# Four PSUM banks in turn for the outputs of every batch of a spectral block, and new homes for the small results that lived in the fourth

## The reference

```python
def spec(x, w1, w2, out_hw):             # rfft2, keep few modes, weight them, irfft2
    xf = rfft2(x, norm='forward')
    top = xf[..., :m1, :m2] * w1; bot = xf[..., H-m1:, :m2] * w2
    return irfft2(place(top, bot), s=out_hw, norm='forward')
def tno(xa):                             # each of 4 x 64 images of 256 x 256 on its own channel
    n = inorm(xa)
    k, q, v = spec(n, kw), spec(n, qw), spec(n, vw)     # 8 x 8 mode blocks
    att = softmax(q . k over the 64 images of a batch) @ v
    att = inorm(att) + xa
    a = inorm(att)
    mixed = inorm(spec(a, mix_w) + skip_w * a)          # 32 x 32 mode blocks
    return inorm(mixed) + att
x = x + tno(group_norm(x))               # x: (4, 64, 256, 256) float32, 32 groups over the columns
```

## Time and profile before

| what | value |
|---|---|
| time, median of 3 runs (lowest, highest) | 711.17 us (709.3, 713.19) |
| the profiled execution: its own time, its span | 708.26 us, 706.2 us |
| PE busy, PEld busy | 659.0 us (93%), 589.9 us (84%) |
| DVE, ACT, POOL busy | 485.6 (69%), 334.8 (47%), 356.8 us (51%) |
| mean granted TensorE clock | 0.979 of full |
| HBM read and written | 68.23 and 67.11 MB |
| `produce` of batches 1 to 3, first store to last landed load | 114.1, 115.5, 114.4 us |

### The profile page before, as it was taken

One profiled execution on the slowest core, in us unless ns is written; L12 is line 12 of the kernel. 1 busy time (PEld: TensorE's weight loads), 2 busy tenths in 40 slices (PEclk: granted clock), 3 DMA queues, 4 the chain that ended last, 5 costly groups with the idle time before them and its releaser, 6 DMA issues.

```text
span 706.2 us, 15104 instructions
## 1 busy us (share of the span) xinstructions
PE 659.0 (93%) x5772; PEld 589.9 (84%) x5772; DVE 485.6 (69%) x1099; ACT 334.8 (47%) x722; POOL 356.8 (51%) x430
## 2 busy tenths in 40 slices
PE   6999998999999998999999989899999999988796
PEld 6999898788888898878888889878888888986574
DVE  3566566678767676577777765867777766656787
ACT  5888041464666513255566633236466660424141
POOL 1700024968980003795993002398699000359995
PEclk9999899999999999999999999999999999999799
DMA  8990000799889500199788910059979970005567
GB/s 265 389 361 3 1 1 2 226 309 296 284 302 301 192 1 1 52 317 328 259 307 289 304 56 1 1 174 316 316 263 304 296 242 1 1 1 209 205 245 297
DMA packets 71687, 136.32 MB, mean 193 GB/s; under 512 B 5376, under 2 KB 5888, under 8 KB 71616
## 3 DMA queue, kind: packets, MB, share of 16 engines
q1 hardware_dynamic: 71616, 135.36, 56.3%
HBM read 68.23 MB, written 67.11 MB: 192 GB/s over the span
## 4 chain that ended last, share of the span: by engine, by line
PE 63%; DVE 14%; POOL 13%; DMA 3%; issue 3%; ACT 2%; SPq 1%; DVEq 0%; ACTq 0%; POOLq 0%
PE psY L306 27%; PE psP L361 13%; POOL X L744 9%; PE psP L417 4%; PE psY L327 4%; PE psT L343 4%; PE psP L327 3%; DVE X L796 3%; DVE Y L796 3%; DVE SQ L796 2%; DMA X<-in_x 2%; DMA out<-X 1%; DVE QP L832 1%; ACT SQ L515 1%; POOL ALPHA L737 1%
## 5 line engine op out<-in xcount | busy, mean ns | idle before, releaser
L744 POOL TENSOR_TENSOR X<-X,ALPHA 128x512 f32<-128x512 f32 x244 | 254.8, 1082 | 27.5 <-DVE IM L1032 25.5
L306 PE MATMUL psY<-FWD,X 128*128 128x128 f32 x2048 | 248.3, 280 | 6.8 <-DMA X<-in_x 6.8
L306 PEld LDWEIGHTS psY<-FWD,X 128*128 128x128 f32 x2048 | 236.7, 194 | 21.5 <-issue 19.1
L796 DVE TENSOR_TENSOR X<-X,psP 128x512 f32<-128x512 f32 x240 | 155.7, 684 | 73.6 <-PE psP L361 60.9
L832 DVE TENSOR_REDUCE QP<-SQ 128x32 f32<-128x512 f32 x256 | 161.8, 679 | 63.4 <-ACT SQ L515 42.2
L361 PE MATMUL psP<-INVW,T 64*128 64x256 f32 x960 | 147.4, 406 | 19.5 <-DVE X L796 16.1
L515 ACT ACTIVATE SQ<-X 128x512 f32<-128x512 f32 x256 | 147.1, 622 | 16.0 <-DVE Y L803 9.1
L722 POOL TENSOR_TENSOR Y<-Y,OMEGA 128x256 f32<-128x256 f32 x32 | 25.3, 790 | 249.6 <-ACT Y L519 249.3
L361 PEld LDWEIGHTS psP<-INVW,T 64*128 64x128 f32 x960 | 94.9, 190 | 51.3 <-issue 39.4
L537 ACT ACTIVATE T<-psT,BIA,SCL 128x256 f32<-128x256 f32 x128 | 65.3, 561 | 116.3 <-PE psT L343 105.3
L507 ACT ACTIVATE Y<-psY 128x512 f32<-128x512 f32 x128 | 76.0, 594 | 66.2 <-PE psY L306 65.6
(11 more groups left out here) (189 smaller groups left out, 463.3 us busy)
## 6 DMA issues: line engine op xcount, KB each, us to landing
X<-in_x SPq DMA_DIRECT2D x128, 512.0 KB, 5.2
out<-X SPq DMA_DIRECT2D x128, 512.0 KB, 4.1
INVH<-t_inv_h SPq DMA_DIRECT2D x1, 256.0 KB, 4.9
LW<-in_low_w SPq DMA_DIRECT2D x1, 204.0 KB, 3.4
GWT<-t_w SPq DMA_DIRECT2D x1, 192.0 KB, 4.9
FWD<-t_fwd SPq DMA_DIRECT2D x1, 128.0 KB, 2.2
INVW<-t_inv_w SPq DMA_DIRECT2D x1, 128.0 KB, 4.7
LM<-in_low_mix SPq DMA_DIRECT2D x1, 68.0 KB, 3.0
```

What stands on the lines that cost most here:

```text
L306: last = mm(psY[p % 2][:, (2 * i + c) * 128:(2 * i + c + 1) * 128], X[:, 2 * p + i, a, c * 128:(c + 1) * 128], FWD[:, a, :], start=a == 0, ...
L744: P.tensor_tensor(v, v, al, MUL).then_inc(x_scaled, 1)
L796: return V.tensor_tensor(out, a, b, op)
```

## The change

Outputs use psP0, psP1, psP2 and psB in turn in all batches, and `inverse_w(s)` waits for image 2s-3 (out_made 2s-2) from s = 2 on; `inverse_w(1)` waits for the first low additions, which read psB. The squares' sums move from psB to the last columns of psT1, with a wait on t_kept. The small results of the second part move from psB to psY1 (psY0 in the last batch). For that, `energy`, `spread` and `turn_low` move behind `inverse_h` in their rounds and wait on y_kept, and the second `forward` of the round after each waits until VectorE has read them. VectorE handles the second part after the third image of a round instead of the fourth. In `attend` the early statistics go to psB instead of psT1.

```diff
...
         psM = [psY[0], psY[1], psP[2]]
-        psTot, psSta, psZ = psT[0], psT[1], psP
+        psTot, psSta, psZ = psT[0], psB, psP
         psA, psQ = psT[1], psP[0]
-        psE = [psT[1], psB]
+        psS = psT[1][:, 480:496]
...
         def out_bank(b, n):
-            return (psP + [psY[0]])[n % 4] if b == B - 1 else psP[n % 3]
+            return (psP + [psB])[n % 4]
+
+        def second_bank(b):
+            return psY[1] if b < B - 1 else psY[0]
+
+        def coef_bank(b, part):
+            return second_bank(b) if part else psT[1]
+
+        def low_bank(b, part):
+            return second_bank(b) if part else psB
...
             q = n // 4 - 4
-            return psY[1][:, GROUPS * q:GROUPS * q + 1] if q < 6 else psB[:, GROUPS * (q - 6):GROUPS * (q - 6) + 1]
+            return psY[1][:, GROUPS * q:GROUPS * q + 1] if q < 6 else psY[0][:, GROUPS * (q - 6):GROUPS * (q - 6) + 1]
...
+                if nb:
+                    pe.wait_ge(t_kept, 32 * (nb - 1) + min(2 * (k + LAG + 1) + 2, 32))
...
                 quad = QP[:, 4 * (k % 2):4 * (k % 2) + 4, :].rearrange("p i g -> p (i g)")
-                mm(psB[:, 480 + k:481 + k], quad, ONES[:, 0:1], start=True, stop=True).then_inc(q_added, 1)
+                mm(psS[:, k:k + 1], quad, ONES[:, 0:1], start=True, stop=True).then_inc(q_added, 1)
...
                     pe.wait_ge(mode_weighted, 8 * b + 6)
-                if b == B - 1 and s == 1:
-                    pe.wait_ge(mode_weighted, 8 * b + 7)
-                    pe.wait_ge(powers, 8 * b + 7)
-                if s:
-                    pe.wait_ge(out_made, 64 * b + 2 * s - (2 if b == B - 1 else 1))
+                if s == 1:
+                    pe.wait_ge(d_added, 6 * b + 4)
+                if s > 1:
+                    pe.wait_ge(out_made, 64 * b + 2 * s - 2)
...
                 pe.wait_ge(energy_part, 10 * b + (6, 10)[part])
-                mm(psE[part][0:IMGS, 496:497], FPH, ONES[:, 0:1],
+                mm(coef_bank(b, part)[0:IMGS, 496:497], FPH, ONES[:, 0:1],
...
                 pe.wait_ge(coef_made, 2 * b + part + 1)
-                mm(psE[part][:, 320:416], SIDE[:, :], RC, start=True, stop=True)
-                mm(psE[part][:, 416:480], ONES[0:IMGS, :], E2, start=True, stop=True).then_inc(coef_spread, 1)
+                mm(coef_bank(b, part)[:, 320:416], SIDE[:, :], RC, start=True, stop=True)
+                mm(coef_bank(b, part)[:, 416:480], ONES[0:IMGS, :], E2, start=True, stop=True).then_inc(coef_spread, 1)
...
                 j0, j1 = (0, 4 * SPLIT) if part == 0 else (4 * SPLIT, 32)
-                wait_alone(d_made, 2 * b + part + 1, psB)
+                wait_alone(d_made, 2 * b + part + 1, low_bank(b, part))
...
                         for h in range(2):
-                            last = mm(psB[64 * h:64 * h + LU, col:16 * (j1 - j0):16], vals, EI[:, 2 * j0 + h:2 * j1:2],
+                            last = mm(low_bank(b, part)[64 * h:64 * h + LU, col:16 * (j1 - j0):16], vals, EI[:, 2 * j0 + h:2 * j1:2],
...
                         forward(b + 1, 2 * (u - LAG))
+                        if u == LAG + 1:
+                            pe.wait_ge(var_made, 2 * b + 2)
+                        if u == LAG + 4:
+                            pe.wait_ge(c2_kept, 2 * b + 2)
+                        if u == LAG + 5:
+                            pe.wait_ge(d_added, 6 * b + 6)
                         forward(b + 1, 2 * (u - LAG) + 1)
-                    if u == LAG:
-                        energy(b, 1)
-                    if u == LAG + 1:
-                        pe.wait_ge(var_made, 2 * b + 2)
-                    if u == LAG + 3:
-                        spread(b, 1)
-                    if u == LAG + 4:
-                        pe.wait_ge(c2_kept, 2 * b + 2)
-                        turn_low(b, 1)
-                    if u == LAG + 5:
-                        pe.wait_ge(d_added, 6 * b + 6)
...
                             inverse_h(b, u + 1)
+                        if new and u in (LAG, LAG + 3, LAG + 4):
+                            pe.wait_ge(y_kept, 32 * (b + 1) + 2 * (u - LAG) + 2)
+                        if u == LAG:
+                            energy(b, 1)
+                        if u == LAG + 3:
+                            spread(b, 1)
+                        if u == LAG + 4:
+                            turn_low(b, 1)
...
                     act.wait_ge(d_added, 6 * b + 6)
+                    act.wait_ge(powers, 8 * b + 8)
...
                 dve.wait_ge(q_added, 16 * b + 16)
-                step(V.tensor_reduce(SUMS[:, 2:3], psB[:, 480:496], AX.X, ADD))
+                step(V.tensor_reduce(SUMS[:, 2:3], psS, AX.X, ADD))
                 ts(TOT[:, 32:64], SEL[:, :], SUMS[:, 2:3], None, MUL).then_inc(totals_in, 1)
-                tt(PAD.rearrange("p (k i) -> p k i", i=4), over(psB[:, 480:481], [[1, 16], [0, 4]]),
+                tt(PAD.rearrange("p (k i) -> p k i", i=4), over(psS[:, 0:1], [[1, 16], [0, 4]]),
...
                 dve.wait_ge(energy_sum, 2 * b + part + 1)
-                step(ts(im(28), psE[part][0:IMGS, 496:497], im(30), 0.0, ADD, ALU.max))
+                step(ts(im(28), coef_bank(b, part)[0:IMGS, 496:497], im(30), 0.0, ADD, ALU.max))
...
                 p0, p1 = ((0, 4 * SPLIT), (4 * SPLIT, PAIRS))[part]
-                ps = psE[part]
+                ps = coef_bank(b, part)
...
                     s = S[rows, q0:q1, 0, :, :].rearrange("p q j (r v) -> p q (j r) v", r=2)[:, :, :, 0:LV]
-                    d = psB[rows, 32 * (q0 - base):32 * (q1 - base)].rearrange("p (q n v) -> p q n v", n=4, v=LV)
+                    d = low_bank(b, n > 1)[rows, 32 * (q0 - base):32 * (q1 - base)].rearrange("p (q n v) -> p q n v", n=4, v=LV)
...
                             finish(b, n)
-                            if n % 4 == (3 if more else 1):
+                            if n % 4 == (2 if more else 1):
...
             def second_part(b, u, more):
```

## The result

| | before | after |
|---|---|---|
| time, median of 4 runs of each side by side | 711.08 us (709.3 to 713.19) | 690.75 us (687.99 to 692.2) |
| ratio, 95% interval | | 0.971 (0.966 to 0.975) |
| profiled execution: time, span | 708.26, 706.2 us | 689.49, 687.4 us |
| `produce` of batches 1 to 3, first store to last landed load | 114.0, 115.4, 114.4 us | 108.1, 109.9, 109.3 us |
| last batch, first store to the end | 70.05 us | 68.62 us |

The forecast was 695.5 us. The two profiled executions are 18.8 us apart: 16.5 in the three `produce` stages, 1.4 in the last batch, and 0.8 before the first store of batch 1 (at 126.5 against 127.3 us), which the change doesn't aim at. The three later `attend` stages take 165.0 us together in both.

The account below looks back on a forecast made before the run. TensorE, busy 93%, was taken as bound by its order and the joint's wait, with transfers second. Terms summed to 15.6 us: 692.7 us profiled, 695.5 us as median; forecast 692 to 701, wider range 690.0 to 704.8 us.

Parts of the forecast that it names:

- (d): Rounds 0 to 2: forward starts about 2.2 us earlier, only 0.7 usable before pair 1's load; 2.1 us in three batches.
- (f): New waits of energy, spread, turn_low and second forwards for banks or VectorE: -0.6 us in three batches.
- (a): Joint of inverse_h and second inverse_w, rounds 3 to 14: wait gone, 36 x 0.33 = 11.9 us.
- (b): Round 8: the 0.82 us beyond the usual joint goes, as inverse_w(17) needs image 31, not 32; 2.4 us.
- (c): Round 15: output of pair 31 comes 0.75 us sooner per batch; 2.2 us in three batches.
- (e): Loads and slower transfers take back 0.9 us in batch 1 and 3.0 at batch ends: -3.9 us.
- (g): Last batch: inverse_w(14) and inverse_h(8) run in the hole before turn_low; 1.5 us, capped by GpSimd's scalings.
- the joint isn't the wait: Rival: the gap before the second inverse_w comes from the banks' change; 6.5 us gained, 704.7 us; chance 0.06.
- Transfers become the bound: Rival: 308 GB/s holds everywhere, a steady round takes 6.81 us; 7.0 us gained, 704.2 us; chance 0.13.
- Nothing is left: Rival: batch ends depend on store and load alone, so TensorE's gain is waited away; 709 to 711 us; chance 0.08.
- The clock falls: Rival: new TensorE stops each bring 6 us of half clock; slower by over 0.5% from seven places; chance 0.06.
- a sign of being wrong: Granted clock of 0.50 inside rounds 3 to 15 was listed among the signs that the prediction is wrong.

Follow-up runs that it names:

- second comparison: The changed kernel, unaltered, run again beside the kernel before and the one with the earlier last store: 692.04 us, ratio 0.975.
- half stores: Only the first 256 of each partition's 512 numbers per image stored: 678.04 us from the changed kernel, 705.55 us from the kernel before.
- strict wait: Changed kernel, but inverse_w in batches 1 to 3 waits as before (out_made 2s-1 in place of 2s-2): 702.26 us, ratio 0.988.
- single images: Changed kernel with the last four pairs of a batch loaded and stored image by image, each with its own semaphore: 706.86 us, ratio 0.995.

## Why the prediction was right, point by point

The mechanism that the prediction rests on, the looser wait at the joint, is what the experiments show. The time is less well hit than that: the median of 690.75 us lies below the 692 to 701 us that the forecast gave itself, and 0.75 us above the low end of the wider range; in the second comparison it was 692.04 us, 17.7 below the kernel before. That the sum comes within 3 us is in part luck, since (d) and (f) came out 2.1 and 2.2 us better than predicted and (a) and the batches' ends 0.7 and 1.3 us worse.

The measured side is from the two traces, three batches together; "round" is from one round's first forward to the next's.

| term | predicted | measured |
|---|---|---|
| (a) joints | 11.9 | 11 a batch x 0.34 = 11.2 |
| (b) round 8 beyond the joint | 2.4 | 3 x 0.81 = 2.4 |
| (c) round 15, with (e) at the batch's end | 2.2 - 3.0 = -0.8 | 3 x 1.21 - 5.7 = -2.1 |
| (d) rounds 0 to 3, with (e) in batch 1 | 2.1 - 0.9 = 1.2 | 3 x 2.26 - 3.4 = 3.3 |
| (f) rounds 6 and 7 beyond the joint | -0.6 | 3 x 0.54 = 1.6 |
| (g) last batch | 1.5 | 1.4 |
| not predicted: before the first store | 0 | 0.8 |
| sum | 15.6 | 18.6 (18.8 by the times) |

(a) **The mechanism** is shown from both sides: the looser wait gives 0.86 us at the joint, the old wait in the same layout gives 1.10 back. The size was right too where the joint stands alone: 0.34 us in rounds 4, 5 and 9 to 14, against 0.33. In rounds 6 and 7 the 0.34 is bookkeeping, see (f). Round 3's joint lies in the stop for the load, so it is counted in (d).

(b) **Round 8** lost its stop as forecast, and the reason I gave, the wait on image 31, is enough for it: with VectorE's old order and the looser wait the stop is gone, and the round is down from 7.86 us (moved parts alone) to 7.04. What I missed is a second cause that is nearly enough by itself: with the old wait and VectorE's new order the round is 7.14 us. The two overlap. Alone they bring 0.82 and 0.72 us, together 1.18 (6.68), so how much "belongs" to either depends on which is counted first. What VectorE's order adds to the looser wait, 0.36 us, is the second forward's new wait for the low additions.

(c), (e) **The batch's end.** TensorE gained 1.21 us in round 15. From the forward of pair 28 to the last landed load it then needed 7.8, 8.4 and 8.1 us, 24.3 in all against 18.6. The two together cost 2.1 us in place of 0.8. I had the loads' delay too small (1.0 us a batch against 1.9), but of the right kind: with half stores the same stretch takes 6.0, 5.8 and 6.4 us. The share of the window ahead gave no sign of it: at 0.94 no forward of rounds 9 to 14 waited, and the last pairs, which have no slack, paid. The Trainium skill, "DMA: Bandwidth & Descriptors", Specifications, puts the limit at 358 GB/s; rounds 0 to 6 of batch 1 were at 0.99 of the DMA engines with 330 GB/s, and halving the stores gained 9.0 us, so head room by that figure was not to be had with loads and stores mixed. Loads alone moved 389 GB/s (last section), above it.

(d) **The start.** `forward` begins 7.68 us after the first store instead of 9.94, 2.26 earlier (2.2 forecast). It used more of that than the 0.7 us a batch: round 3 grew by 0.4, 1.6 and 1.5 us. In batches 2 and 3 the estimate held to 0.1 us. In batch 1 the load of pair 1 came sooner and 1.9 us of the gain stayed. The loss of 0.9 us before round 6 of batch 1 isn't to be found: round 4 took 0.09 us more than the others.

(f) **The moved parts** is the term with the wrong sign. I looked only at the new waits, and none showed: in round 7 the trace has no stop before L380. What I missed is that a piece of work placed in a joint where an engine would wait anyway is hidden there. `spread` and `turn_low` ran between the forwards and `inverse_w` at their full price, and now they stand where VectorE's addition is awaited. The kernel with only these moves has rounds 6 and 7 shorter by 0.54 us each, and so has the one with the strict wait. In the changed kernel the two rounds are 0.68 and 0.54 us shorter; less two joints of 0.34, counted in (a), 0.54 us a batch is left. That split is bookkeeping: with the moves and the strict wait round 7 already takes the 8.19 us that it takes in the changed kernel, and round 6 takes 7.26 against 7.12. The moves and the looser wait shorten the same joint, so beside the moves the wait brought 0.14 us in round 6 and nothing in round 7, and the two gains don't add up there.

(g) **The last batch** came out at 1.4 us, and with the moved parts alone it was already 68.60 us. VectorE meets GpSimd at 677.75 us, the cap that was given. The half clock of the earlier trace rows, which stood behind the stop of 2.52 us, is gone as well: the granted clock of the changed kernel is 1.00 in these rounds. How much of VectorE's stops of 2.10 and 1.22 us it had caused isn't separated. It doesn't show in the stage: the kernel with the early rounds' looser wait has half clock twice for 3.4 us in its last batch, and needs 68.6 us too.

Of the **rivals**, "the joint isn't the wait" fell with the strict wait. "Transfers become the bound" would have needed a steady round of 6.81 us; it was 6.68 in rounds 9 to 14, and in the first trace only rounds 3 and 4 and the batches' ends lost time to transfers. "Nothing is left" would have needed all to be given back at the ends; they gave back 5.7 us of over 20. "The clock falls" was real as a mechanism but too rare: one such stop in the second trace of the changed kernel, one at the end of batch 3 in the kernel with the earlier last store, one at the end of batch 1 with the strict wait, at 1.6 us each, and none in the first trace; only the single images, with their longer stops, had more. It would take seven. The one in the second trace lies inside round 3, which the prediction had named as a sign of being wrong. The forwards' waits for loads also passed the 8 to 14 us that it had given, with 15.0 us in the first trace and 18.3 in the second.

The 0.8 us before the first store is not explained by the change: the kernel before has half clock there from 113.8 to 117.2 us and the changed one doesn't, and in all traces together the first store comes at 124.1 to 127.8 us. The later `attend` stages cancel, since one of them takes 56.1 us in either trace (see below). The median fell by 20.3 us, 1.5 more than the profiled executions, which is within the spread of the runs (3.9 and 4.2 us).

## What to carry to other kernels

When an instruction starts a little after the end of another engine's work on the bank it reuses, count the banks: one more bank in the rotation lets the wait reach back to work that ended a round ago. Before you price small work that is moved, ask what the engine does at its new place; in a joint with a wait of its own it costs little (`spread` 0.25 us in place of 0.58), and the saving at the old place is real. But two gains at the same joint don't add up. A faster round draws the same bytes in less time: look not at the mean share but at the one transfer without slack, here the last of each batch and the first that the earlier start asks for.

## What the runs showed of the hardware

**The clock after a stop of about 2 us.** After stops of TensorE of 1.48 us (above), and of 1.92 us at the end of batch 1 with the early rounds' looser wait, the clock stayed whole. After 2.14 us (above), 2.01 us at the end of batch 1 with the strict wait, and 2.10 us in the kernel with the earlier last store, it was at half for 3.4 us. The last of these:

```profile
558.40 3.65 PE L317 MATMUL psY<-FWD,X 128*128 128x128 f32 x16 [2.10 <-DMA X<-in_x]
```

Sixteen matmul instructions took 3.65 us here, and 2.05 us with the whole clock. The `attend` stages behind batches 1 and 2 each have a stop near this length, and the clock fell in one of two that look alike:

```profile
275.53 0.28 PE L384 MATMUL psT<-ONES,Y 128*64 128x1 f32 x2 [1.97 <-DVE Y L810]
```

```profile
441.47 0.28 PE L384 MATMUL psT<-ONES,Y 128*64 128x1 f32 x2 [1.96 <-DVE Y L810]
```

The first stands in batch 2's `attend`, with half clock from 276.1 to 279.5 and 56.1 us in all; the second in batch 3's, with the clock whole throughout and 54.5 us. Stages of 54.5 and 56.1 us turn up in traces of the old and the changed kernel alike, so 1.6 us per batch of any comparison of two single traces can come from there. What decides it is open.

**Transfers.** In the row of GB/s of the profile's page, by slice of 17.2 us, the second and third slice of the changed kernel are loads alone:

```profile
GB/s 265 389 383 11 1 1 1 190 324 341 295 320 311 181 1 1 14 303 330 315 315 317 310 61 1 1 146 316 299 342 308 313 241 1 1 2 214 200 298 268
```

They moved 389 and 383 GB/s; with stores beside them 322 to 330 GB/s was the most over a window of some 40 us, at 0.98 and 0.99 of the DMA engines. A load of 256 KB took 4.0 us where one of 512 KB took 5.4.
